# Cross attention's chain, setup products, division and weight split re-placed, and the last scaling done on VectorE alone

## The chip, the cores and the metric

The kernel runs on one core of one Trainium2 chip. The metric is the device time of one execution in microseconds (us), the slowest core's, which here is the only one. Three runs of the kernel before gave 744.47 to 745.14 us, median 744.66.

## What is computed

Two transformer layers in a row, on x of shape 2 x 1024 x 256 in float32 with a context of 2 x 77 x 256:

```python
# layer 0, 16 heads of 16, scale 64 ** -0.5
x = attention(ln(x), ln(x), Wq1, Wkv1, Wo1, bo1) + x      # self attention, 1024 keys
x = attention(ln(x), context, Wq2, Wkv2, Wo2, bo2) + x    # cross attention, 77 keys
lin, gelu = split(ln(x) @ Wff1 + bff1)                    # 256 -> 2 x 1024
x = (lin * gelu * sigmoid(1.702 * gelu)) @ Wff2 + bff2 + x
# layer 1, one head of 256, keys and values from the context
Q, K, V = x @ Wq.T + bq, ctx @ Wk.T + bk, ctx @ Wv.T + bv
out = softmax(Q @ K.T / 16) @ V @ Wfc.T + bfc
x = norm_w * rms_normalised(out + x)
```

## The kernel before, in words

The order of the work is written out by hand: each engine has its own program, and the engines meet at semaphores. "TensorE" is PE in the rows, "VectorE" DVE, "ScalarE" ACT, "GpSimd" POOL, "SyncE" SP. The tokens are 16 tiles of 128 rows, or 4 blocks of 512. Everything stays in SBUF but for the parts of the projected queries and keys, which go to DRAM and come back in another layout (`q_parts`, `k_parts`).

**Self attention** has 8 groups (one group is 4 heads of one batch entry) of 16 steps each. TensorE makes scores for the row maxima (L760), which VectorE reduces (L1562), then transposed scores (L926), ScalarE takes their exponential (L1324) and TensorE weighs the values with it (L938). It reads the values from the tile `v1`. GpSimd has almost nothing to do here: from the fourth half group on it splits the maxima into two float16 parts (L663 to L667), for which it waits 13 times.

**Cross attention** has 8 groups of 4 units. I number the units 0 to 31, unit 4 G + d being `cross_unit(G, d)`. In a unit TensorE makes transposed scores (L1034, `scores_t2`) and, 6 units ahead (`S2_LEAD`), a tile of scores for the maxima (L1023, `scores_2`). There are 32 such tiles. VectorE reduces each (L1764, `reduce_2`), and TensorE makes no tile before the one ahead of it is reduced. After every fourth tile VectorE splits the group's maxima (L1568, L1570) and TensorE turns them (L1061, `turn_max_2`) in the third unit of a group. ScalarE takes the exponential (L1379), TensorE weighs the values (L1043) in a group's first and third unit and turns the result back (L1054) in the second and fourth, and VectorE divides it by the sums (`attended`, L1713 and L1719).

Between these pieces stand two more kinds of work, which the change moves:

- The **chain** (`chain(n, b)`): after attention n of batch entry b come 2 transposes of the attention's output (L713), 8 output products (L901), each added to x by VectorE (L1657) with its statistics (L1531, L1532), and for each block a transpose of the normalised tokens (L713), in self attention's chain followed by 2 projections of the queries (L727). A `yield` ends one piece. The table `PIECES` says how many pieces a unit gets. The normalisation between (root in 12 small instructions, then four `tok` writes, L1540) is drawn out over the units by `tick(3)`, three instructions each time. TensorE takes half of a unit's pieces in the middle of the unit (rounded down) and the rest at its end.
- The **setup products** of layer 1 (`final_setup`, `setup`, L843): kT and vT (two each), g1 (two), cb, and vw (one for each batch entry, after which SBUF holds V @ Wfc.T + bfc). Seven of them are made just ahead of the score tiles numbered in `SETUP_TILES`, in columns 312 onward of the score tiles' PSUM banks, which the score tile leaves free (`SPARE`). The two vw products are 256 columns wide, more than is free there, so they wait for all score tiles and come after units 28 and 30 (`SETUPS`).

```python
PIECES = ((2, 1, 1, 1), (1, 1, 1, 1), (0, 0, 0, 0), (0, 0, 0, 0),
          (0, 0, 1, 1), (2, 1, 2, 1), (1, 1, 0, 1), (0, 1, 0, 0))
SETUP_TILES = (10, 14, 15, 17, 19, 21, 23)
SETUPS = {(7, 0): 1, (7, 2): 1}
```

**The feed-forward part** works on products of split operands: each float32 weight is split into a high and a low part. GpSimd does this for the second weight (`wff2_hi`, `wff2_lo`, L628, L630, four pairs of instructions), after the bias of the cross attention and once self attention no longer reads `v1`, where `wff2_hi` lies; then, once all query parts are stored, for the first (L637, L639, eight pairs). The first block's input is split by ScalarE (`x_high(0)`, L1364, after unit 28) and VectorE (`x_low(0)`, L1753, after unit 29).

**The tail** is layer 1's attention over 77 keys, the residual (L1848), sums of squares on ScalarE (L1454), a reciprocal root on VectorE (`l1_root`, 12 instructions) and the scaling. Block 0 is scaled on ScalarE (`l1_scale`, L1460) and GpSimd (L672), blocks 1 to 3 on VectorE (`l1_final`, L1860). SyncE stores the blocks in the order 0, 1, 3, 2 (L575).

## Time and profile before

| what | value |
|---|---|
| median of three runs | 744.66 us |
| the profiled execution's own time | 745.36 us |
| its span, first to last instruction | 743.5 us |
| TensorE busy | 670.9 us (90%) |
| VectorE busy | 534.5 us (72%) |
| ScalarE busy | 486.2 us (65%) |
| GpSimd busy | 92.8 us (12%) |
| chain that ended last | TensorE 66%, VectorE 18%, ScalarE 9% |

The profile is of one execution. The span is shorter than the execution's own time by the 1.9 us that lie around it. Busy shares are averages over stages with different limits, so the stages are read one by one. The granted clock is TensorE's: 1.00 is 2.4 GHz, 0.50 is 1.2 GHz. The chain that ended last is followed back from the last instruction, at each step to what released it.

### The profile page before, as it was taken

To read this page: it belongs to the slowest core of one execution; us is meant where nothing else is said; L and a number is where in the kernel's file an instruction comes from. 1 tells how busy PE (TensorE), PEld (TensorE's weight loads), DVE (VectorE), ACT (ScalarE), POOL (GpSimd) and SP (SyncE) were. 2 spreads that over 40 slices of the span, in tenths; PEclk is the share of its full clock that TensorE was granted. 3 is DMA by queue.
4 is the path that set the end of the run, shared out by engine and by line. 5 is a ranking of instruction groups with operands and counts; after the bars stand their busy time and mean duration, and the time that the engine had idled before them with its cause. 6 is when DMAs were issued, how large, how long until landed. Compare 5 with 4: busy or idle time off the path is not lost.

```text
span 743.5 us, 11151 instructions
## 1 busy us (share of the span) xinstructions
PE 670.9 (90%) x4072; PEld 321.4 (43%) x4072; DVE 534.5 (72%) x925; ACT 486.2 (65%) x845; POOL 92.8 (12%) x144
## 2 busy tenths in 40 slices
PE   4989799999999999999999888989989989999991
PEld 2644122222222222222224344344547878888881
DVE  6778999999999999999984538453753844343357
ACT  3542399999999999999998653444674223332374
POOL 2080800000000000000000201570000050000001
PEclk9999599999999999999999999865999999999996
DMA  9557450202020110101000031120000000000003
GB/s 305 195 178 240 100 185 5 69 1 71 1 72 2 44 30 1 30 2 30 1 2 1 29 89 27 55 69 24 2 2 1 0 1 1 1 1 1 1 0 113
DMA packets 35113, 36.87 MB, mean 50 GB/s; under 512 B 6132, under 2 KB 28276, under 8 KB 34804
## 3 DMA queue, kind: packets, MB, share of 16 engines
q1 hardware_dynamic: 33904, 35.87, 15.2%
q0 software_dynamic: 1024, 0.24, 0.3%
q8 instruction: 32, 0.52, 0.3%
q14 instruction: 21, 0.17, 0.1%
q10 hardware_dynamic: 132, 0.07, 0.0%
HBM read 23.09 MB, written 12.74 MB: 48 GB/s over the span
## 4 chain that ended last, share of the span: by engine, by line
PE 66%; DVE 18%; ACT 9%; issue 5%; DMA 1%; SPq 0%; DVEq 0%; ACTq 0%
PE ps L938 15%; PE ps L926 10%; DVE mm L1562 7%; PE ps L727 6%; ACT probs L1324 6%; PE ps L1127 4%; PE ps L1128 4%; PE ps L1129 4%; PE ps L760 4%; PE ps L713 3%; PE ps L1043 3%; PE ps L901 2%; PE ps L1143 2%; PE ps L1142 2%; PE ps L1144 2%
## 5 line engine op out<-in xcount | busy, mean ns | idle before, releaser
L1324 ACT ACTIVATE probs<-ps,unfit 128x512 f32<-128x512 f32 x512 | 311.7, 691 | 29.1 <-PE ps L926 24.6
L1562 DVE TENSOR_REDUCE mm<-ps 128x2 f32<-128x1024 f32 x256 | 299.5, 1219 | 14.4 <-PE ps L760 10.4
L926 PE MATMUL ps<-stack 50*128 50x512 f16 x512 | 147.2, 389 | 7.2 <-ACT probs L1324 1.2
L938 PE MATMUL ps<-probs,v 128*32 128x512 f32 x1024 | 137.6, 609 | 2.7 <-ACT outT L1329 2.7
L760 PE MATMUL ps<-stack 48*128 48x512 f16 x512 | 109.1, 392 | 12.6 <-DVE mm L1562 6.6
L926 PEld LDWEIGHTS ps<-stack 50*128 50x128 f16 x512 | 36.9, 93 | 172.9 <-ACT probs L1324 164.8
L1424 ACT ACTIVATE early<-ps,cols 128x512 f32<-128x512 f32 x32 | 22.1, 690 | 93.1 <-PE ps L1129 93.1
L1822 DVE SCALAR_TENSOR_TENSOR hid<-ps,cols,early 128x512 f32<-128x512 f32 x32 | 24.0, 750 | 74.3 <-PE ps L1129 74.3
L621 POOL TENSOR_TENSOR x<-x,rows 128x512 f32<-128x512 f32 x24 | 30.9, 1314 | 164.8 <-PE ps L1129 91.4
L1127 PE MATMUL ps<-x_hi,wff_hi 128*128 128x512 f32 x128 | 51.3, 401 | 0.1
L1379 ACT ACTIVATE probs<-ps,unfit 96x1024 f32<-96x1024 f32 x32 | 35.5, 1108 | 23.2 <-PE ps L1034 23.2
L1128 PE MATMUL ps<-x_lo,wff_hi 128*128 128x512 f32 x128 | 50.3, 393 | 0.0
L1129 PE MATMUL ps<-x_hi,wff_lo 128*128 128x512 f32 x128 | 50.2, 392 | 0.0
L760 PEld LDWEIGHTS ps<-stack 48*128 48x128 f16 x512 | 26.1, 94 | 54.3 <-DVE mm L1562 30.5
L713 PE MATMUL ps<-ident,tok 128*128 128x128 f32 x160 | 27.0, 313 | 18.2 <-DVE tok L1540 13.9
L663 POOL TENSOR_SCALAR mu<-mm 128x16 f32<-128x16 f32 x13 | 3.3, 254 | 286.9 <-DVE mm L1578 286.9
L938 PEld LDWEIGHTS ps<-probs,v 128*32 128x32 f32 x1024 | 20.6, 108 | 40.7 <-issue 30.8
L1142 PE MATMUL ps<-wff_hi,hid_hi 128*128 128x256 f32 x128 | 37.2, 290 | 0.0
L1143 PE MATMUL ps<-wff_lo,hid_hi 128*128 128x256 f32 x128 | 36.6, 286 | 0.0
L1144 PE MATMUL ps<-wff_hi,hid_lo 128*128 128x256 f32 x128 | 36.2, 283 | 0.0
L901 PE MATMUL ps<-wo,wkv 128*128 128x256 f32 x128 | 33.6, 398 | 2.2 <-DVE x L1657 1.6
L1764 DVE TENSOR_REDUCE mm<-ps 128x8 f32<-128x616 f32 x32 | 25.3, 790 | 11.5 <-PE ps L1023 11.2
(168 smaller groups left out, 863.8 us busy)
## 6 DMA issues: line engine op xcount, KB each, us to landing
v_groups<-early SPq DMA_DIRECT2D x8, 512.0 KB, 3.4
stack<-q_parts SPq DMA_DIRECT2D x64, 64.0 KB, 2.0
v<-v_groups SPq DMA_DIRECT2D x8, 512.0 KB, 4.1
x<-in_x SPq DMA_DIRECT2D x4, 512.0 KB, 7.6
q_parts<-probs SPq DMA_DIRECT2D x8, 256.0 KB, 3.8
k_parts<-probs SPq DMA_DIRECT2D x8, 256.0 KB, 2.5
stack<-k_parts SPq DMA_DIRECT2D x16, 128.0 KB, 2.5
stack<-q_parts SPq DMA_DIRECT2D x64, 32.0 KB, 1.9
```

What stands on the lines that cost most here:

```text
L713: mm_ = eng.transpose(ps[:, turn_bank(phase, blk, c), P * t:P * t + P], src, ident[:, :])
L760: mm_ = eng.matmul(ps[:, 2 * s_slot(G, j, i) + tile, :], qs[rows_i, slot, half, q, P * t:P * t + P], stack[rows_i, SLOTS + slot, q, BLK * ...
L926: eng.matmul(ps[:, st_bank(n), :], stack[rows_of(tile, KROWS), SLOTS + slot, q, P * kc:P * kc + P], qs[rows_of(tile, KROWS), slot, half, q ...
L938: mm_ = eng.matmul(ps[32 * h:32 * h + 32, PV, :], v1[:, G % 2, kc, 32 * h:32 * h + 32], probs[:, k % 2, h, :], start=(kc == 0), stop=(kc = ...
L1127: eng.matmul(ps[:, bank, :], wh, xh[:, c, :], start=(c == 0), stop=False)
L1128: eng.matmul(ps[:, bank, :], wh, xl[:, c, :], start=False, stop=False)
L1129: mm_ = eng.matmul(ps[:, bank, :], wl, xh[:, c, :], start=False, stop=(c == NC - 1))
L1142: eng.matmul(out, hh, w2h, start=(f == 0), stop=False)
L1143: eng.matmul(out, hh, w2l, start=False, stop=False)
L1144: mm_ = eng.matmul(out, hl, w2h, start=False, stop=(f == FC - 1))
L1324: eng.activation(probs[:, k % 2, HEADS[h], :], ps[:, st_bank(n), :], ACT.Exp, scale=unfit[:, 0:1]).then_inc(exp_done, 1)
L1562: eng.tensor_reduce(dst, ps[:, 2 * slot:2 * slot + 2, :], AX.X, ALU.max).then_inc(s_red, 1)
```

## The change

Six edits:

1. `PIECES` gives one piece to each unit that has any. A piece leaves unit 0 for unit 8; in the second chain the eight output products come one per unit in units 20 to 27, and the two last transposes in units 29 and 31 in place of 27 and 29. `x_high(0)` comes after unit 30 and `x_low(0)` after unit 31.
2. The setup products come ahead of the tiles 14 to 24, in units 8 to 18, one each. vw is made in halves of 128 columns so that all fit in the spare columns; there are 11 products in place of 9.
3. In a unit VectorE divides the attention's output before the three instructions of `tick(3)`, and no further `tick(3)` follows a division.
4. GpSimd splits the second weight in self attention, between the loads of k2 and the first maxima. `wff2_hi` lies over `p1T`, which only the tail uses, and `p1T` is no longer cleared at the start. The tail's products over `p1T` read 77 rows in place of 96.
5. VectorE alone scales all four blocks: block 0 after the residual of block 3, then one root for blocks 1 to 3 and their twelve instructions.
6. SyncE stores the blocks in the order 0 to 3.

```diff
-        wff2_hi, wff2_lo = over("wff2_hi", "v1", [P, FC, D], F32R), over("wff2_lo", "wff2", [P, FC, D], F32R)
+        wff2_lo = over("wff2_lo", "wff2", [P, FC, D], F32R)
...
+        wff2_hi = over("wff2_hi", "p1T", [P, FC, D], F32R)
...
-        PIECES = ((2, 1, 1, 1), (1, 1, 1, 1), (0, 0, 0, 0), (0, 0, 0, 0),
-                  (0, 0, 1, 1), (2, 1, 2, 1), (1, 1, 0, 1), (0, 1, 0, 0))
-
-        SETUP_TILES = (10, 14, 15, 17, 19, 21, 23)
-        SETUPS = {(7, 0): 1, (7, 2): 1}
+        PIECES = ((1, 1, 1, 1), (1, 1, 1, 1), (1, 0, 0, 0), (0, 0, 0, 0),
+                  (0, 0, 1, 1), (1, 1, 1, 1), (1, 1, 1, 1), (0, 1, 0, 1))
+
+        SETUP_TILES = range(14, 25)
...
-            for n, blk in enumerate((0, 1, BLOCKS - 1, 2)):
-                if n == 0:
-                    eng.wait_ge(l_out, TPB)
-                else:
-                    eng.wait_ge(l_last, TPB * n)
+            for blk in range(BLOCKS):
+                eng.wait_ge(l_last, TPB * (blk + 1))
...
                 if n == 1:
-
-                    eng.wait_ge(w_in["wff"], 32)
-                    eng.wait_ge(pv_done, 16 * GROUPS)
-                    for f in range(0, FC, 2):
...
+                    eng.wait_ge(w_in["wff"], 32)
+                    for f in range(0, FC, 2):
+                        hi, w = wff2_hi[:, f:f + 2, :], wff2[:, f:f + 2, :]
+                        eng.tensor_copy(hi, w).then_inc(w2_split, 1)
...
-                eng.wait_ge(s2_red, KC // 2 * GROUPS)
                 for b in range(B):
-                    setup(k, CTX, D, [(vT[:, c, cut[b]], wfcT[:, c, :]) for c in range(NC)]
-                          + [(ones[0:1, 0:CTX], rows[0:1, ROW_BFC, :])])
-                    k += 1
-                    yield
+                    for n in (slice(0, P), slice(P, D)):
+                        setup(k, CTX, P, [(vT[:, c, cut[b]], wfcT[:, c, n]) for c in range(NC)]
+                              + [(ones[0:1, 0:CTX], rows[0:1, ROW_BFC, n])])
+                        k += 1
+                        yield
...
-                    if (G, d) == (LAST, 0):
+                    if (G, d) == (LAST, 2):
                         x_high(0)
...
             def attended_2(G, half):
                 attended(2 * GROUPS + 2 * G + half, MISC)
-                tick(3)
...
-                tick(3)
-                advance(pieces, PIECES[G][d] // 2)
                 if d == 1 and G >= 1:
                     attended_2(G - 1, 1)
                 if d == 3:
                     attended_2(G, 0)
-                advance(pieces, PIECES[G][d] - PIECES[G][d] // 2)
+                tick(3)
+                advance(pieces, PIECES[G][d])
...
-                    if (G, d) == (LAST, 1):
+                    if (G, d) == (LAST, 3):
                         x_low(0)
...
-            l1_root(1, 2)
-            l1_final(1, 2)
-            l1_root(2, BLOCKS)
-            l1_final(last, 3)
-            l1_final(2, 3)
+            l1_final(0, 1)
+            l1_root(1, BLOCKS)
+            for blk in range(1, BLOCKS):
+                l1_final(blk, 2)
```

Three places of the order, before and now. Line numbers of the change differ from those before.

The first is VectorE in units 0 and 1. Before, from the output product added in the middle of unit 0 to the reduction of the next score tile in unit 1 (`x<-ps,x` is the sum of an output product and x, `rstd` and `var` the root, `tok` the normalised tokens, `mm` the maxima):

```order
L1657 TENSOR_TENSOR x<-ps,x 128x256
L1531 BN_STATS st<-x 128x6
L1532 BN_AGGR mv<-st 128x2
L1514 TENSOR_TENSOR var<-rstd 128x4
L1514 TENSOR_TENSOR var<-var,half_var 128x4
L1517 SCALAR_TENSOR_TENSOR rstd<-var,rstd 128x4
L1657 TENSOR_TENSOR x<-ps,x 128x256
L1531 BN_STATS st<-x 128x6
L1532 BN_AGGR mv<-st 128x2
L1540 TENSOR_SCALAR tok<-x,mv,rstd 128x256 x3
L1764 TENSOR_REDUCE mm<-ps 128x2x2x2
```

Now, from the same output product:

```order
L1637 TENSOR_TENSOR x<-ps,x 128x256
L1511 BN_STATS st<-x 128x6
L1512 BN_AGGR mv<-st 128x2
L1494 TENSOR_TENSOR var<-rstd 128x4
L1494 TENSOR_TENSOR var<-var,half_var 128x4
L1497 SCALAR_TENSOR_TENSOR rstd<-var,rstd 128x4
L1744 TENSOR_REDUCE mm<-ps 128x2x2x2
L1548 TENSOR_SCALAR mpart<-mm 128x2x16
L1550 SCALAR_TENSOR_TENSOR mpart<-mm,mpart 128x2x16
L1520 TENSOR_SCALAR tok<-x,mv,rstd 128x256 x3
```

One output product with its statistics and three `tok` writes no longer stand ahead of that reduction.

The second is TensorE in units 10 and 11, where no chain pieces are. Before (`ps<-stack,k` the transposed scores, `ps<-k,stack` the score tile, `identh,mpart` the turned maxima, `probs,v` the weighing, `ctxT,early` a setup product, `ident,outT` the turned output):

```order
L1034 MATMUL ps<-stack,k 96x512 x2
L1023 MATMUL ps<-k,stack 128x78 x8
L1061 MATMUL ps<-identh,mpart 96x128
L1043 MATMUL ps<-probs,v 32x512 x4
L1034 MATMUL ps<-stack,k 96x512 x2
L843 MATMUL ps<-ctxT,early 128x154 x2
L1023 MATMUL ps<-k,stack 128x78 x8
L1054 MATMUL ps<-ident,outT 128x128 x4
```

Now:

```order
L1022 MATMUL ps<-stack,k 96x512 x2
L831 MATMUL ps<-ctxT,early 128x154 x2
L1011 MATMUL ps<-k,stack 128x78 x8
L1049 MATMUL ps<-identh,mpart 96x128
L1031 MATMUL ps<-probs,v 32x512 x4
L1022 MATMUL ps<-stack,k 96x512 x2
L831 MATMUL ps<-ctxT,early 128x154 x2
L1011 MATMUL ps<-k,stack 128x78 x8
L1042 MATMUL ps<-ident,outT 128x128 x4
```

Unit 10 has a setup product too, ahead of its score tile; so have all units from 8 to 18, where before every second one had.

The third is TensorE at the end of cross attention, units 29 to 31 up to the feed-forward part's first product (`ps<-x_hi...`). Before, from unit 29:

```order
L1034 MATMUL ps<-stack,k 96x512 x2
L1054 MATMUL ps<-ident,outT 128x128 x4
L713 MATMUL ps<-ident,tok 128x128 x8
L1034 MATMUL ps<-stack,k 96x512 x2
L1043 MATMUL ps<-probs,v 32x512 x4
L843 MATMUL ps<-early,vT 77x256 x2
L843 MATMUL ps<-rows,ones 77x256
L1034 MATMUL ps<-stack,k 96x512 x2
L1054 MATMUL ps<-ident,outT 128x128 x4
L1043 MATMUL ps<-probs,v 32x512 x4
L1127 MATMUL ps<-x_hi_55,wff_hi 128x512
```

Now, units 29 to 31:

```order
L1022 MATMUL ps<-stack,k 96x512 x2
L1042 MATMUL ps<-ident,outT 128x128 x4
L702 MATMUL ps<-ident,tok 128x128 x8
L1022 MATMUL ps<-stack,k 96x512 x2
L1031 MATMUL ps<-probs,v 32x512 x4
L1022 MATMUL ps<-stack,k 96x512 x2
L1042 MATMUL ps<-ident,outT 128x128 x4
L702 MATMUL ps<-ident,tok 128x128 x8
L1031 MATMUL ps<-probs,v 32x512 x4
L1114 MATMUL ps<-x_hi_54,wff_hi 128x512
```

The vw products are gone from here, and the second transpose of the normalised tokens (`ident,tok`) has moved from unit 29 to unit 31, the last.

## Rows read from the trace of the kernel before

**Rows 1.** The page's first line
```profile
span 743.5 us, 11151 instructions
```

**Rows 2.** Busy time by stage, columns in the first line
```profile
core 0: us, PE busy (x) PEld busy (x) DVE busy (x) ACT busy (x) POOL busy (x), PEclk, DMA share, GB/s
450.70:462.30 11.60, 8.65 (x62) 4.90 (x63) 10.72 (x42) 4.96 (x6) 2.63 (x2) 0.87 0.10 24
462.30:482.80 20.50, 19.06 (x108) 8.19 (x107) 10.33 (x27) 10.72 (x15) 10.11 (x10) 0.82 0.13 41
490.00:520.40 30.40, 28.81 (x165) 13.88 (x166) 11.66 (x25) 13.15 (x18) 11.88 (x13) 0.50 0.13 35
520.40:545.00 24.60, 21.61 (x178) 12.48 (x174) 20.04 (x70) 14.75 (x19) 0.00 (x0) 0.99 0.01 2
555.20:715.40 160.20, 155.86 (x912) 136.88 (x909) 72.94 (x149) 55.83 (x99) 10.55 (x8) 0.99 0.00 1
715.40:743.50 28.10, 12.23 (x75) 10.16 (x73) 19.94 (x73) 15.69 (x60) 2.78 (x4) 0.80 0.22 75
```

**Rows 3.** The same view, two short stretches of units 0 to 7
```profile
459.60:462.30 2.70, 2.70 (x15) 1.58 (x12) 2.33 (x11) 1.35 (x2) 0.69 (x1) 0.50 0.03 6
473.00:479.50 6.50, 6.50 (x27) 2.24 (x25) 0.95 (x2) 3.22 (x5) 6.13 (x7) 0.50 0.13 33
```

**Rows 4.** Timeline of TensorE: start, duration, line, operands, [idle before]
```profile
458.09 0.32 PE L1023 MATMUL ps<-k,stack 48*128 48x78 f16 x8 [2.15 <-DVE mm L1764]
...
489.86 0.23 PE L1061 MATMUL ps<-identh,mpart 128*96 128x128 f16 x1 [1.74 <-DVE tok L1719]
...
554.18 1.06 PE L1043 MATMUL ps<-probs,v 96*32 96x512 f32 x8 [0.62 <-ACT probs L1379]
```

**Rows 5.** One line's instructions on VectorE (ns, min/median/max, first and last start)
```profile
L1570 DVE SCALAR_TENSOR_TENSOR mpart<-mm,mpart x11: 174/193/1183, 77.0 to 540.5; 128x32 f16<-128x32 f32 x8, 128x16 f16<-128x16 f32 x3
```

**Rows 6.** Timeline of GpSimd, start of the first weight's split
```profile
487.09 0.61 POOL L637 CAST wff_hi<-wff 128x512 fp32r<-128x512 f32 x1 [5.23 <-DMA q_parts<-stack]
```

**Rows 7.** Chain of waits: start, us, work
```profile
483.25 0.72 PE ps L843 x4
...
506.16 1.32 PE ps L843 x4
...
507.86 1.04 PE ps L1054 x4
...
546.28 1.60 PE ps L843 x6
```

**Rows 8.** Timeline of ScalarE: exponentials of units 10 and 19
```profile
487.51 1.11 ACT L1379 ACTIVATE probs<-ps,unfit 96x1024 f32<-96x1024 f32 x1 [0.63 <-PE ps L1034]
...
520.88 1.12 ACT L1379 ACTIVATE probs<-ps,unfit 96x1024 f32<-96x1024 f32 x1
```

**Rows 9.** Timeline of VectorE at the end of cross attention
```profile
545.68 1.06 DVE L1540 TENSOR_SCALAR tok<-x,mv,rstd 128x256 f32<-128x256 f32 x3
...
549.48 1.22 DVE L1753 TENSOR_TENSOR x_lo<-xT,x_hi 128x1024 fp32r<-128x1024 f32 x1
```

**Rows 10.** Timeline of VectorE in the tail
```profile
730.24 0.64 DVE L1509 TENSOR_SCALAR half_ms<-ms 128x4 f32<-128x4 f32 x1
...
732.90 1.67 DVE L1860 SCALAR_TENSOR_TENSOR x<-x,rms,rows 128x256 f32<-128x256 f32 x4
...
736.90 3.26 DVE L1860 SCALAR_TENSOR_TENSOR x<-x,rms,rows 128x256 f32<-128x256 f32 x8
```

**Rows 11.** Timeline of SyncE's queue, load of the second weight
```profile
92.91 0.47 SPq L507 DMA_DIRECT2D wff<-in_Wff  x1
```

**Rows 12.** DMA issues: name, KB each, us to landing
```profile
wff<-in_Wff SPq DMA_DIRECT2D x1, 1024.0 KB, 10.4
```

**Rows 13.** Timeline of VectorE in self attention
```profile
118.41 0.18 DVE L1580 TENSOR_TENSOR mm<-mm 128x16 f32<-128x16 f32 x1
```

**Rows 14.** Groups by line: us in total, mean ns, idle before
```profile
L630 POOL TENSOR_TENSOR wff_lo<-wff,wff_hi 128x512 fp32r<-128x512 f32 x4 | 5.1, 1270 | 0.3
```

45 lines of the change are left out of this document (14 added, 31 removed).

## The prediction

> **What bounds the kernel now.** I read busy time by stage first. The span is 743.5 us [rows 1]. The feed-forward stretch of 160.2 us has TensorE busy for 155.86 us at full clock, and the change touches nothing in it. Self attention gains one thing, the second weight's split on GpSimd. That leaves cross attention (450.7 to 555.2) and the tail after 715.4. The reader should see in [rows 2] that three stages of cross attention have three limits. In units 0 to 3 VectorE is busy 10.72 of 11.60 us. From 490.0 to 520.4 TensorE is busy 28.81 of 30.40 us, but at a granted clock of 0.50, which is 1.2 GHz. From 520.4 to 545.0 both are near full (21.61 and 20.04 of 24.60). So the largest thing at stake is not an amount of work but 30.4 us at half clock, with 2.7 and 6.5 us more at half clock before it [rows 3].
>
> I then looked at what TensorE did ahead of the falls. Before 459.6 it had stood 2.15 us, waiting for a score tile's reduction. Before 490.0 it had stood 1.74 us, waiting for the maxima and the division [rows 4]. In that second wait lies one VectorE instruction, the low half of the maxima, that took 1183 ns where the median is 193 [rows 5]. It fell into the time just after GpSimd had started to split the first weight at 487.09 [rows 6]. TensorE did not come back to full clock until a transpose of the chain, at 520.4. The trace shows only that order of events; that the waits cause the falls is my reading.
>
> **The change part by part.**
>
> *Units 0 to 8, one piece each.* Between two reductions of score tiles VectorE has three `tok` writes (1.06 in [rows 9]), one addition of an output product and its statistics fewer, an estimated 2 us, about the size of the 2.15 us wait. VectorE's total work until unit 3 is the same, at 92% busy, so most of this wait will spread over the next units and not vanish. What can go is the 2.7 us stretch at half clock behind it: at full clock it is 1.35 us shorter. I take -1.4. Best case, both half-clock stretches go (half of 9.2 is 4.6) with the wait: -6.8. Worst case, the transpose that moves to unit 6 now finds its four `tok` writes just being made, 4 x 0.35 = 1.4: +1.4. Dividing first brings the division forward by three small instructions, about 0.5 us, in units with a root under way. TensorE waits on it there only in a group's third unit; I count it within these bounds.
>
> *Units 8 to 19, a setup product in each to 18.* Units 10 to 19 run from 487.51 to 520.88, 33.4 us for nine units [rows 8], the last with a transpose. How much work moves in: from unit 11 on there were four wide products, and there will be four wide ones and four halves. A wide one costs 0.72 at full and 1.32 at half clock; a vw whole costs 1.60 [rows 7]. A half has six records of 128 columns; the transposes of 128 columns take 1.04 / 4 = 0.26 each at half clock [rows 7], so a half is 1.56 there, and about 0.85 at full. Four halves add 6.2 at half clock, 3.4 at full.
> At full clock the stretch would hold 28.81 / 2 + 3.4 = 17.8 us of TensorE's work, two group waits of 1.74 (3.5) and a wait of 0.62 for an exponential in every second unit (2.8) [rows 4], together 24.1, so -9.3. At half clock all the way it grows by the halves: +6.2. These are the ends. Which is nearer? What stood ahead of the fall was a pause of 1.74 us in unit 10 with no other work for TensorE. Now unit 10 has a product of 0.72 to fill the same wait, and the slow VectorE instruction should be quick there. The reason is that GpSimd starts the first weight only when the last query parts are stored, 487.09 [rows 6], and their projection moves from unit 7 to unit 8, so unit 9's maxima come first. The collision then meets unit 13's maxima, whose wait also has a product in it. I expect full clock for most of the stretch with one fall like the 6.5 us at 473.0 [rows 3], which costs 3.3: -9.3 + 3.3 = -6.0.
>
> *Units 20 to 31.* The same VectorE work is spread evenly. Two vw products go (3.20), but ScalarE is busy there too with its copies, and I count half, -1.6. Against it, the last block's transpose now stands in unit 31: its four `tok` writes (1.4), and then `x_low(0)` (1.22) [rows 9], come behind the last division, and the feed-forward part waits for both. Before, TensorE had its last output turned at 554.18 - 0.62 = 553.56, and 1.06 us of weighing from 554.18 on ended the stage [rows 4], so 1.7 us in all. Now come a division (an estimated 0.7), the `tok` writes (1.4), the part of the transpose left after the last of them (about 0.7 of twice 0.52, [rows 7]) and the weighing (1.06), 3.9. That is +2.2. Sum +0.6, ends -3.2 and +2.2.
>
> *The tail.* One root goes (from 734.57 to 736.90, 2.33), four scalings come (1.67), and the instruction of 0.64 that ran beside GpSimd's product becomes about 0.2 like other small ones [rows 5]: -2.33 + 1.67 - 0.44 = -1.1 [rows 10]. Block 0 leaves later, but the last two blocks leave one behind the other as before, so the last store is not later relative to the last scaling. Ends -1.6 (ScalarE's four scalings also gone from ahead of its squares) and 0 (three stores closer together).
>
> *The second weight's split.* Its load is issued at 92.91 and lands 10.4 us later [rows 11, 12], and four pairs of 1.27 and 0.61 take 7.5 us [rows 6, 14], so it runs from about 103.3 to 111. VectorE's next work on SBUF operands begins at 118.41 [rows 13], and GpSimd's own first maxima come with the fourth half group, much later. Cover: over 5 us. I count 0, ends 0 and +1 (a slowed VectorE instruction in a stage that ScalarE bounds). At its old place nothing waited for it: the next split waited for stored parts until 487.09 anyway. The `p1T` clearing and the 77 rows change no duration on the path: 0.
>
> **Sum.** -1.4 - 6.0 + 0.6 - 1.1 = -7.9. Against the profiled execution's 745.36 this is 737.5. The median of the runs is 0.7 lower, so I forecast **736.8**.
>
> **Rivals.**
> *A, no half clock left in units 10 to 19.* For it: TensorE has a product in every wait. Against it: three falls in 40 us before. -1.4 - 9.3 + 0.6 - 1.1 = -11.2, 733.5; with the first term's best case, 728.
> The Trainium skill, "TensorE: Matmul & The Clock Gate", Part 1, says that the clock is low after idleness and is released by sustained activity. By that rule a denser TensorE is released early and rival A is the outcome. The trace agrees on the falls, which follow waits, and speaks against the second half: 28.81 of 30.40 us busy and no release [rows 2]. So A does not get the largest share.
> *B, the fall only comes later.* Units 11 to 14 at full clock save about 4.5 us, and the four halves still fall in the half-clock part (+6.2). Sum -1.4 + 1.7 + 0.6 - 1.1 = -0.2: no change. With one of the halves at full clock it is -1 to -4.
> *C, slower: the half-clock stretch stays as long and has four more products in it.* Its place is units 11 to 19 on TensorE, its price +6.2. It decides as soon as the clock falls before unit 12, since nothing but chain work was seen to end such a stretch. Sum -1.4 + 6.2 + 0.6 - 1.1 = +4.3, 749.0. For it: half-clock TensorE stayed busy and at 0.50 with products in every second unit.
> *D, one piece per unit does nothing*, because VectorE is the limit in units 0 to 3 and 20 to 27 and its work is unchanged. The clock is then drawn as before. Its times are those of B and C.
>
> **How the numbers follow.** About 0.2% (1.5 us) is what a measurement of this kernel can tell from no change. The forecast's case (-4 to -9.5) gets 0.37, A 0.18, B 0.20 (half of it within 0.2%, half slightly faster), C with what is slower in D 0.25. Faster is 0.37 + 0.18 + 0.10 = 0.65, same 0.10, slower 0.25. The range reaches into A and C: 730.0 to 749.5. The forecast's own case spans 735 to 741.
>
> **What would show each step.** The 2.15 us wait of TensorE gone and the half-clock stretch at 459.6 with it; the share of 0.50 between units 10 and 19 well under half; the slow maxima instruction in unit 13 and not in unit 9; a wait of TensorE for `tok` in unit 31 of 1 to 2 us; the last scaling ending about 1 us earlier relative to the last residual; self attention as long as before. Wrong would be: the half-clock stretch still 25 us or more, or a new half-clock stretch at the start of the feed-forward part.

## The result, and the profile after

The changed kernel was slower: median 750.38 us (748.30 to 751.27, eight runs) against 743.40 us (738.93 to 745.14, eight runs) of the kernel before, ratio 1.0107, 95% interval 1.0077 to 1.0137. That is 13.6 us over the forecast of 736.8 and 0.9 us over the end of the range, 749.5. Its profiled execution took 750.86 us (span 748.8), against 745.36 (span 743.5) before. Runs of one kernel differ mostly by how long TensorE ran at half clock (one kernel below took 730.82 us at a mean granted clock of 0.974 and 746.57 us at 0.947), so I set medians beside what each profile shows of the clock; the ratios leave out runs over 1.5% above the fastest of their kernel, which leaves two of the four runs of e5 below, and of e2 and e3 only one each, so that they have no ratio.

Busy time by stage of the changed kernel, columns as in [rows 2]:

```profile
451.90:462.30 10.40, 8.26 (x74) 4.83 (x73) 9.78 (x38) 5.44 (x7) 2.65 (x2) 1.00 0.10 28
462.30:482.80 20.50, 17.75 (x113) 7.70 (x112) 12.87 (x34) 11.76 (x16) 2.64 (x2) 0.92 0.15 50
492.90:526.60 33.70, 31.20 (x168) 15.47 (x170) 9.75 (x24) 11.73 (x15) 9.95 (x11) 0.50 0.09 28
526.60:549.60 23.00, 21.39 (x178) 11.62 (x172) 18.87 (x61) 14.87 (x20) 0.00 (x0) 0.99 0.01 2
557.80:561.00 3.20, 3.20 (x12) 1.34 (x12) 0.30 (x1) 2.21 (x4) 0.00 (x0) 0.50 0.00 0
559.70:719.80 160.10, 155.91 (x901) 136.51 (x898) 72.22 (x146) 54.61 (x93) 10.54 (x8) 0.97 0.00 1
719.80:748.80 29.00, 13.46 (x85) 11.39 (x83) 19.98 (x67) 15.43 (x63) 0.00 (x0) 0.76 0.22 73
```

Units 0 to 3 now run at full clock (1.00, before 0.87 in [rows 2]), and the stretch behind them is at 0.92, before 0.82. But the long half-clock stretch has not shortened: it was 30.4 us and is 33.7. A new one of 3.2 us stands at the start of the feed-forward part. What stands ahead of the long one, and in it, is on TensorE's timeline (start, duration, work, [idle before]):

```profile
489.97 0.66 PE L1042 MATMUL ps<-ident,outT 128*128 128x128 f32 x4
495.40 0.66 PE L1022 MATMUL ps<-stack,k 50*96 50x512 f16 x2 [4.78 <-DMA stack<-mT]
...
507.90 1.14 PE L831 MATMUL ps<-early,vT 128*77 128x128 f32 x4
508.97 0.71 PE L831 MATMUL ps<-rows,ones 1*77 1x128 f32 x2
...
524.07 1.97 PE L702 MATMUL ps<-ident,tok 128*128 128x128 f32 x8
```

The wait of 1.74 us at unit 10 [rows 4] is gone. In its place TensorE stands 4.78 us at unit 12, for the DMA that brings group 3's maxima (`mT`) into the stack. Where these maxima were is seen on ScalarE's timeline (their copy), in SyncE's queue, and in the chain of waits (start, us, work):

```profile
487.77 0.27 ACT L1359 ACTIVATE mT<-ps 64x128 f16<-64x128 f32 x1 [0.58 <-PE ps L1049]
```
```profile
481.10 4.60 SPq L440 DMA_DIRECT2D q_parts<-stack  x2
485.74 7.02 SPq L456 DMA_DIRECT2D stack<-q_parts  x12
492.81 1.28 SPq L528 DMA_DIRECT2D stack<-mT  x2
```
```profile
488.90 1.54 SPq L456 DMA_DIRECT2D stack<-q_parts  x1
```
```profile
493.47 1.89 DMA stack<-mT
```

They were ready at 488.04 (487.77 + 0.27) and issued from 492.81: SyncE first issues twelve query loads, eight of them only after the last query parts are stored. One of these twelve alone, the line at 488.90, took 1.54 us to issue, where most take about 0.4; what held it is not shown. The same load in the kernel before, where TensorE came to unit 12 at half clock and did not wait:

```profile
490.80 1.28 SPq L531 DMA_DIRECT2D stack<-mT  x2
```

The span is split here at events that both timelines show; "unit" is the start of that unit's exponential on ScalarE:

| stretch | before | after | difference | forecast |
|---|---|---|---|---|
| up to unit 0 | 451.15 | 452.37 | +1.22 | 0 |
| unit 0 to 9 | 34.63 | 32.04 | -2.59 | -1.4 |
| unit 9 to 12 | 10.15 | 11.70 | +1.55 | |
| unit 12 to 19 | 24.95 | 30.57 | +5.62 | with the line above -6.0 |
| unit 19 to the feed-forward part | 34.29 | 33.00 | -1.29 | +0.6 |
| feed-forward part to the last residual | 174.96 | 176.08 | +1.12 | 0 |
| last residual to the last scaling | 10.03 | 9.61 | -0.42 | -1.1 |
| last scaling to the end | 3.34 | 3.43 | +0.09 | 0 |
| sum | 743.5 | 748.8 | +5.30 | -7.9 |

At the end of cross attention, VectorE and TensorE in unit 31:

```profile
552.46 0.16 DVE L1497 SCALAR_TENSOR_TENSOR rstd<-var,rstd 128x4 f32<-128x4 f32 x1
554.96 0.26 DVE L1693 RECIPROCAL rec<-ps 128x16 f32<-128x16 f32 x1 [2.34 <-PE ps L1042]
555.26 0.42 DVE L1699 TENSOR_TENSOR tok<-ps,rec 128x256 f32<-128x256 f32 x1
555.60 1.37 DVE L1520 TENSOR_SCALAR tok<-x,mv,rstd 128x256 f32<-128x256 f32 x4
```
```profile
556.15 1.74 PE L702 MATMUL ps<-ident,tok 128*128 128x128 f32 x8 [1.22 <-DVE tok L1520]
```

The root was done at 552.62. Then VectorE stood 2.34 us for the division's input, with the four `tok` writes queued behind the division, because the third edit puts the division first. TensorE waited 1.22 us for them.

The tail on VectorE, which answers to [rows 10]:

```profile
734.10 1.66 DVE L1825 SCALAR_TENSOR_TENSOR x<-ps,r,x 128x256 f32<-128x256 f32 x4
735.68 1.66 DVE L1837 SCALAR_TENSOR_TENSOR x<-x,rms,rows 128x256 f32<-128x256 f32 x4
738.07 0.17 DVE L1489 TENSOR_SCALAR ms<-ss 128x12 f32<-128x12 f32 x1 [0.72 <-ACT sq L1441]
...
740.53 4.84 DVE L1837 SCALAR_TENSOR_TENSOR x<-x,rms,rows 128x256 f32<-128x256 f32 x12
```

One root is gone, but VectorE now stands 0.72 us for ScalarE's squares.

### The profile page after: what moved, and what is told of

Same layout as the page of the kernel before. It is cut to its first block, busy times and chain, and to the rows that moved or that the text cites. A ratio compares the mean times of both kernels' runs of the same rounds, so it can differ in the third digit from the quotient of the medians.

```text
span 748.8 us, 11160 instructions
## 1 busy us (share of the span) xinstructions
PE 674.0 (90%) x4084; PEld 323.9 (43%) x4084; DVE 533.8 (71%) x919; ACT 484.8 (65%) x841; POOL 88.4 (12%) x139
## 4 chain that ended last, share of the span: by engine, by line
PE 66%; DVE 16%; ACT 10%; issue 5%; DMA 1%; SPq 1%; DVEq 0%; ACTq 0%
PE ps L926 15%; PE ps L914 10%; DVE mm L1542 7%; PE ps L716 6%; ACT probs L1311 5%; PE ps L1114 4%; PE ps L1115 4%; PE ps L1116 4%; PE ps L749 4%; PE ps L702 3%; PE ps L889 3%; PE ps L1031 2%; PE ps L1131 2%; PE ps L1129 2%; PE ps L1130 2%
## 5 line engine op out<-in xcount | busy, mean ns | idle before, releaser
L702 PEld LDWEIGHTS ps<-ident,tok 128*128 128x128 f32 x160 | 20.4, 155 | 28.3 <-issue 19.7
```

The source lines that it names most:

```text
L702: mm_ = eng.transpose(ps[:, turn_bank(phase, blk, c), P * t:P * t + P], src, ident[:, :])
```

## Experiments

All sixteen ran beside runs of the kernel before on the same chip; "before" is the median of those. The last column is from each run's profile.

| run | median (range), runs | before | ratio, 95% interval | unit 12 to 19, us |
|---|---|---|---|---|
| e1 maxima ahead of the last loads | 750.29 (747.47-751.12), 5 | 743.44 | 1.010 (1.0065-1.0134) | 30.5 |
| e2 maxima from ScalarE | 743.59 (730.82-746.57), 4 | 743.44 | - | 28.3 |
| e3 setup placement alone, on before | 749.24 (735.60-751.03), 4 | 743.44 | - | 30.6 |
| e4 second chain as before | 754.93 (751.13-758.49), 4 | 743.44 | 1.0169 (1.0112-1.0225) | 30.6 |
| e5 e2 and GpSimd in two lots | 739.51 (733.57-747.55), 4 | 743.79 | 0.9876 (0.9817-0.9936) | 19.1 |
| e6 eight transposes added | 741.50 (738.53-744.23), 10 | 743.79 | 0.9973 (0.9943-1.0003) | 22.2 |
| e7 three products added | 742.10 (738.58-746.22), 10 | 743.79 | 0.9991 (0.9957-1.0025) | 23.3 |
| e8 division after the root | 746.95 (744.86-748.68), 10 | 743.79 | 1.0054 (1.0028-1.0080) | 30.6 |
| e9 e5, e8 and e6 together | 733.91 (728.49-736.42), 6 | 743.86 | 0.9870 (0.9828-0.9912) | 19.2 |
| e10 setup placement undone | 741.99 (739.46-744.85), 10 | 743.86 | 0.9979 (0.9953-1.0005) | 24.5 |
| e11 eight transposes on before | 744.90 (739.80-745.61), 12 | 743.86 | 1.0010 (0.9983-1.0038) | 23.0 |
| e12 transposes twice | 732.68 (729.40-742.06), 6 | 743.86 | 0.9853 (0.9812-0.9893) | 28.2 |
| e13 two lots, on before | 741.34 (738.25-745.30), 12 | 743.62 | 0.9980 (0.9957-1.0003) | 24.2 |
| e14 three edits (e5 and e8) | 731.32 (728.08-733.46), 5 | 743.62 | 0.9835 (0.9809-0.9862) | 18.7 |
| e15 e14, setup placement undone | 736.80 (731.85-742.99), 10 | 743.62 | 0.9911 (0.9878-0.9943) | 17.9 |
| e16 both repairs on before | 734.03 (728.62-740.15), 6 | 744.12 | 0.9863 (0.9809-0.9916) | 16.3 |

### e1 and e2: is the new wait the queue's?

```diff
 load_q2(4, (1,))
-load_q2(5, (1,))
 load_max_2(3)
+load_q2(5, (1,))
```

> The changed kernel with one move in SyncE's queue: the two loads of group 3's maxima go ahead of the last four query loads. In the changed kernel TensorE stood 4.78 us at unit 12 for these maxima, which were issued at 492.81 although ScalarE had copied them some 4 us before. Theory Q (the wait is the queue's, and the half clock from 492.9 on follows from it): the load is issued some 1.7 us earlier, the wait shrinks to about 3 us, and the time falls by 1.7 us at least, to about 748.7. The clock still falls behind a 3 us wait. Theory F (TensorE loses its clock in these units by itself, whatever it waits for): the clock falls at the same place, and the time falls by the same 1.7 us or less. Rival W (the wait is for the copy or the product of the maxima, not for the queue): the wait stays above 4 us and the time at 750.4. A new wait is possible at the first tile that reads the four query loads, unit 14's: under 1 us.

```diff
 # ScalarE, behind its copy of the maxima; SyncE no longer has load_max_2(3)
+if G == 3:
+    eng.wait_ge(m_copied, 2 * GROUPS + G + 1)
+    n = PARTS * HP * KC
+    for tile in range(HT):
+        eng.dma_start(stack[max_rows(tile), Q2_SLOT[G % 4], :, :].rearrange("i h n -> i (h n)"),
+                      mT[n * tile:n * tile + n, G % 2, :]).then_inc(m2_in[G % 4], 16)
```

> The changed kernel, but the two loads of group 3's maxima are issued by ScalarE itself right behind its copy of them, in unit 10, and not by SyncE behind its query loads. Theory Q: the wait of 4.78 us at unit 12 falls under 1 us. If the clock then holds, units 12 to 18 run in some 20 us in place of 31, and the time falls by 10 us or more, to 740 or less; if it falls at another wait before unit 14, the time falls by about the 4 us of the wait, to 746. Theory F says the latter: the stretch at 0.50 begins in these units anyway and ends only at the chain's transpose in unit 18. Rival W: nothing changes, the wait is still over 4 us.

TensorE in e1, then in e2 with a window of e2, and GpSimd and VectorE in e2:

```profile
493.29 0.66 PE L1022 MATMUL ps<-stack,k 50*96 50x512 f16 x2 [2.51 <-DMA stack<-mT]
```
```profile
498.07 0.23 PE L1048 MATMUL ps<-identh,mpart 128*96 128x128 f16 x1 [1.42 <-DVE tok L1704]
```
```profile
498.20:518.60 20.40, 20.40 (x108) 9.80 (x109) 6.28 (x15) 7.32 (x10) 4.03 (x5) 0.51 0.09 22
```
```profile
495.43 1.27 POOL L622 TENSOR_TENSOR wff_lo<-wff,wff_hi 128x512 fp32r<-128x512 f32 x1
```
```profile
495.58 1.16 DVE L1553 TENSOR_SCALAR mpart<-mm 128x32 f16<-128x32 f32 x1
496.77 0.53 DVE L1555 SCALAR_TENSOR_TENSOR mpart<-mm,mpart 128x32 f16<-128x32 f32 x1
```

The wait is the queue's: 4.78 became 2.51 with four loads fewer ahead of it, and at unit 12 of e2 no wait for it is left. Rival W is out. But e1's time did not move. Its clock fell all the same, and 1.7 of the 2.1 us that its profile had gained at unit 12 were given back in the feed-forward part, where more of it ran at half clock (from the first product to the last residual 177.75 us, in the changed kernel 176.08). In e2 the clock held through units 12 and 13 and fell at unit 14, behind the next wait: two small VectorE instructions took 1.16 and 0.53 us in place of 0.18 and 0.19 while GpSimd was splitting the first weight. This is the same collision as the 1183 ns of [rows 5], one group of maxima later. The kernel before had this second one too, at half clock, with a wait of 1.21 us behind it at 503.39:

```profile
501.39 1.00 DVE L1568 TENSOR_SCALAR mpart<-mm 128x32 f16<-128x32 f32 x1
```

One run of e2 took 730.82 us at a mean clock of 0.974, so in all likelihood the clock can hold there.

The Trainium skill, "SBUF — State Buffer", section "SBUF: two separate sides", says that VectorE and GpSimd share one pair of ports as an exclusive lock, and that the loser waits for the other's whole instruction; on VectorE it counts only instructions in a two-port mode or with two inputs in SBUF. The times here agree: the slow instruction ended at 496.74, just behind the GpSimd subtraction that ended at 496.70, and the excess, 1.16 - 0.18 = 0.98 us, is under one such subtraction (1.27). The instruction has one input, and no run here shows its mode.

### e5: take the collision away as well

```diff
 for f in range(FC):          # GpSimd, the first weight's split
+    if f == FC // 2:
+        eng.wait_ge(m_step, 3 * ON_DVE + 2 * 5)   # group 4's maxima are split
```

> The kernel of the run before last but one, in which ScalarE issues the loads of group 3's maxima, with one more edit: GpSimd splits the first weight in two lots of four pairs, and begins the second lot only once VectorE has split group 4's maxima. Without this edit the profile showed the next wait of TensorE at unit 14: 1.42 us at 498.07, behind two VectorE instructions of 1.16 and 0.53 us that otherwise take 0.18 and 0.19 and ran while GpSimd was splitting, and the clock fell at about 498.2 and stayed low for 20.5 us. Theory G (this collision makes the wait, and the wait the fall): the two instructions take about 0.2 each, the wait is under 0.3 us, the clock holds through units 12 to 18 in most runs, and the time is 731 to 735. Theory F (the clock falls in these units anyway): the wait goes, the stretch at 0.50 stays 17 to 31 us long, and the time is within 2 us of 743.6.

Units 9 to 19 of e5:

```profile
484.40:510.80 26.40, 24.01 (x228) 13.08 (x227) 15.04 (x38) 15.37 (x21) 14.68 (x16) 1.00 0.24 65
```

Clock 1.00 throughout. Two of four runs took 733.8 and 733.6 us, the others 745.3 and 747.6. Theory G's mechanism is shown in the profile, which is of the run of 733.78 us; "in most runs" was not.

### e3, e10 and e15: the placement of the setup products

e3 puts the second edit alone on the kernel before; e10 undoes it alone in the changed kernel; e15 undoes it in the kernel of three edits (below), with GpSimd's first lot held back behind group 3's maxima as well, as in e13.

```diff
-SETUP_TILES = (10, 14, 15, 17, 19, 21, 23)    # e3; reversed in e10 and e15
-SETUPS = {(7, 0): 1, (7, 2): 1}
+SETUP_TILES = range(14, 25)
```

> The kernel before with the placement of the setup products alone: ahead of tiles 14 to 24, vw in four halves, nothing behind units 28 and 30. Theory C of the prediction (the half-clock stretch stays as long and holds four more products): where the clock falls at unit 10 or before as it did, the stretch up to the transpose of unit 18 grows from 30.4 us to about 36, and the products gone from units 28 and 30 give back up to 3: the time rises by 3 to 6 us over the kernel before. Theory D (dense TensorE work holds the clock): the product in unit 10 covers the 1.74 us wait there, the clock holds, and the time falls by 5 us or more. Rival: the pieces and the queue are the whole loss, and this stands within 1 us of the kernel before.

> The changed kernel with its second edit alone undone: the setup products ahead of the tiles 10, 14, 15, 17, 19, 21 and 23, and the two whole vw products after units 28 and 30. Theory C of the prediction (four more products lie in the half-clock stretch and cost 6 us there): the wait of over 4 us at unit 12 stays, the stretch at 0.50 is 27 to 31 us long in place of 34, and the time falls by 6 less up to 3 for the products at the end, 3 to 6 us: 744.5 to 747. Rival Q (the 4.78 us wait is what costs, not the products): 750 within 1.

The half-clock stretch of e3, and then of e10, with the wait of TensorE ahead of the latter:

```profile
485.50:523.00 37.50, 37.50 (x202) 18.98 (x195) 12.76 (x31) 14.77 (x19) 11.64 (x13) 0.50 0.10 28
```
```profile
488.20:518.90 30.70, 26.25 (x154) 13.22 (x156) 10.79 (x24) 12.56 (x17) 13.57 (x15) 0.50 0.15 40
```
```profile
486.59 0.23 PE L1055 MATMUL ps<-identh,mpart 128*96 128x128 f16 x1 [0.75 <-DVE tok L1706]
```

Theory C holds. e3 has the changed kernel's time without any of its other edits, and without its 4.78 us wait: there the clock fell at unit 10 already, behind a wait of 1.10 us, and the setup products after it were paid at half clock. e10 falls by 8.4 us although it still waits 3.30 us at unit 12. From its unit 12 to 19 it takes 24.5 us against 30.6. That is 6.1 us, and the prediction had priced rival C at 6.2. The median came out under the 744.5 to 747 that I expected; where the rest was gained is open. The clock of e10 fell at 488.2, ahead of the long wait, when TensorE had stood only 0.40 and 0.75 us in unit 10. (One run of e3 took 735.60 us at a clock of 0.968: the fall is likely, not certain.)

> The same three edits on the changed kernel with its setup placement undone (seven products in every second unit, two whole vw products after units 28 and 30). Theory H (the new placement costs only where the clock is low, and holds the clock where it is high): this one loses the clock more often and is slower than the kernel of three edits in its fast group, 736 or more. Theory C alone (products in these units cost, and do nothing for the clock): it is as fast or faster, 730 to 733.

With the waits mended, the sign is the other: e15 is slower than e14 in the median, 736.80 against 731.32. Where the clock holds, the placement itself is worth little: in both profiles it held over nearly all of units 9 to 19, e15 took 0.9 us less there (25.20 against 26.05) and 1.0 us more from unit 19 to the feed-forward part, and the spans differ by 1.7 us. The rest of the difference goes with the clock: five of e15's ten runs had a mean clock of 0.956 or less, no run of e14 had under 0.967. That fits a placement that helps to keep the clock, as the prediction assumed, but it is not shown: e5, with the new placement, lost it in two of four runs (0.950 and 0.945), and e16, with the old one, in one of six (0.956). What is shown is that the placement is paid dearly once the clock is lost.

### e6, e7 and e11: what gives the clock back?

```diff
+if (G, d) == (3, 1):          # end of unit 13; e11: (2, 3), unit 11
+    eng.wait_ge(rest_done, len(PROJ))
+    for t in range(2 * TPB):
+        eng.transpose(ps[:, CHAIN + t // TPB, P * (t % TPB):P * (t % TPB) + P], ident[:, :], ident[:, :])
```

e7 has three pairs of products of `wkT` with `ctxT` in that place.

> The changed kernel with eight transposes of the identity added on TensorE at the end of unit 13, into two PSUM banks that nobody reads; their results are used by nothing. In all profiles so far the half-clock stretch of units 12 to 18 ended in the chain's eight transposes of unit 18. Theory T (work of that kind, or an uninterrupted stretch of it, gives the clock back): the stretch begins at 492.9 as before, ends within unit 13 or 14, is 7 to 14 us long in place of 34, and the time falls by (34 - 10) / 2 less 1 to 2 for the transposes, 10 us: about 740. Theory U (the clock comes back by its own time, whatever is done): the stretch stays over 27 us, and the time rises by the 2 us of the transposes, to 752.

> The twin of the kernel with eight added transposes: in the same place, three products of the setup kind (two matrices of 128 x 128 against 154 columns each, 1.39 us a piece at half clock) in place of the transposes, some 4 us of uninterrupted float32 work. Theory T1 (any dense work gives the clock back): as there, the stretch shrinks to 7 to 14 us, and the time is about 741. Theory T2 (it is the transposes that do it): the stretch stays over 27 us, and the time rises by the 4 us, to 754.

e6's added transposes and the windows around them; then e7's added products:

```profile
503.16 1.41 PE L1070 MATMUL ps<-ident 128*128 128x128 f32 x8
```
```profile
493.60:503.80 10.20, 7.99 (x44) 4.60 (x44) 2.43 (x5) 2.79 (x3) 9.80 (x11) 0.50 0.17 46
503.80:518.70 14.90, 14.49 (x137) 8.01 (x137) 7.45 (x21) 8.56 (x12) 0.04 (x1) 1.00 0.12 30
```
```profile
499.31 2.54 PE L1071 MATMUL ps<-ctxT,early 128*128 128x154 f32 x12
```

In both the stretch is 10.2 us in place of 33.7, and ends inside the added work; the times fall by 8.9 and 8.3 us. Neither kind is special (T2 is out), and in these two kernels it is no matter of time alone (U is out). Work that nobody uses made the changed kernel faster. There TensorE was busy for 31.20 of 33.70 us at 0.50 without release. The Trainium skill ("TensorE: Matmul & The Clock Gate", Part 1) says that sustained activity releases the clock. By that rule it should have come back early here, and it did not. What ends such a stretch stays open. At the end of the long one in the changed kernel, and of those in e6 and e7, TensorE had just made or was making a block of float32 products with 128 x 128 weights: the chain's eight transposes (1.97 us at 524.07), eight added ones, or three added pairs. But two later profiles speak against a rule from that. TensorE in e12, which has eight transposes at the ends of units 12 and 15 (its slowest run, 742.06 us), and then in e15, which has none added:

```profile
492.16 0.79 PE L832 MATMUL ps<-kT,early 128*128 128x154 f32 x4 [1.00 <-DMA stack<-q_parts]
...
494.41 1.97 PE L1071 MATMUL ps<-ident 128*128 128x128 f32 x8
```
```profile
493.80:510.80 17.00, 17.00 (x87) 10.30 (x83) 5.16 (x13) 5.38 (x7) 8.61 (x9) 0.50 0.18 45
```
```profile
499.50:502.90 3.40, 3.40 (x30) 2.29 (x33) 1.86 (x5) 1.54 (x3) 3.24 (x5) 0.50 0.32 82
```

In e12 the first eight transposes did not end the stretch that had just begun; it lasted 17.0 us and ended behind the second eight, which began at 507.63. In e15 a stretch ended after 3.4 us, over the ordinary work of units 15 and 16. So in the changed kernel the added work gave the clock back (all twenty runs of e6 and e7 are under its fastest, 748.30 us), but such a block is neither always enough nor always needed.

> The kernel before, with nothing changed but eight transposes of the identity, which nobody reads, at the end of unit 11. Theory T (an uninterrupted stretch of float32 work gives the clock back): the stretch at 0.50, which begins at 490.0 in unit 10, ends within 10 to 14 us in place of 30.4, and the time falls by (30.4 - 12) / 2 less 2 us for the transposes at half clock, 7 us: 736 to 738. Theory U (what freed the clock in the changed kernel belongs to that kernel): no gain, 745.

TensorE in e11, and the granted clock between:

```profile
489.69 0.23 PE L1061 MATMUL ps<-identh,mpart 128*96 128x128 f16 x1 [1.75 <-DVE tok L1723]
...
494.91 1.89 PE L1082 MATMUL ps<-ident 128*128 128x128 f32 x8
...
503.00 0.23 PE L1061 MATMUL ps<-identh,mpart 128*96 128x128 f16 x1 [1.73 <-DVE tok L1723]
```
```profile
489.85:496.70 6.85, 6.85 (x35) 4.04 (x34) 2.13 (x5) 1.95 (x3) 6.61 (x8) 0.50 0.32 88
496.70:503.10 6.40, 4.32 (x48) 2.20 (x47) 4.02 (x8) 3.81 (x4) 5.24 (x6) 1.00 0.01 2
503.10:520.20 17.10, 16.71 (x100) 8.15 (x99) 5.66 (x13) 7.84 (x12) 0.00 (x0) 0.51 0.09 26
```

The clock came back, and TensorE ran into the collision of unit 14 at full speed: 1.73 us of waiting, and the clock was gone for 17.1 us more. No gain, against my expectation. The two waits stand one behind the other. Curing one handed the fall to the next here.

### e13 and e16: the same two repairs on the kernel before

```diff
+    if f % (FC // 2) == 0:     # GpSimd waits for group 3's, then group 4's maxima
+        eng.wait_ge(m_step, 3 * ON_DVE + 2 * (4 + f // (FC // 2)))
```

> The kernel before with one edit: GpSimd begins the first four pairs of the first weight's split only once VectorE has split group 3's maxima (unit 9), and the other four once it has split group 4's (unit 13). In the kernel before, the maxima instruction of 1183 ns and a wait of TensorE of 1.74 us stood ahead of the fall at 490.0, and with eight transposes added the clock came back at 497 and fell again at 503, behind a second wait of 1.73 us at unit 14. Theory G (the collision with GpSimd makes both waits, and they the falls): both waits go under 1 us, no or a shorter half-clock stretch, time 731 to 738. Theory F (the clock falls there anyway, the units have too little uninterrupted work): the waits shrink, the stretch stays near 30 us, 742 to 745.

TensorE in e13:

```profile
489.44 0.23 PE L1063 MATMUL ps<-identh,mpart 128*96 128x128 f16 x1 [0.75 <-DVE tok L1721]
...
495.42 0.66 PE L1036 MATMUL ps<-stack,k 50*96 50x512 f16 x2 [2.86 <-DMA stack<-mT]
```

The time, 741.34 us, is no change clear of noise (0.9957 to 1.0003) and lies between the two theories' ranges. With the collision gone, the kernel before meets the wait that the changed kernel met. Here too the load of the maxima was late all along, hidden by a TensorE that came later and slower.

> The kernel before with the two repairs and nothing of the change: GpSimd's split in two lots behind VectorE's maxima, and the loads of group 3's maxima issued by ScalarE. With the lots alone the wait of 1.74 us at unit 10 went to 0.75, TensorE stood 2.86 us at unit 12 for the maxima's load instead, the clock fell there at 494, and the time was 741.3. Theory Q+G (these two waits make the half-clock stretch): the wait at unit 12 goes under 0.5 us, the stretch is gone or short in most runs, the median is 733 to 738. Rival F: the units 12 to 18 of the kernel before are too thin to hold the clock (every second unit has no setup product), it falls there in most runs, and the median is 740 to 744.

Units 9 to 19 of e16:

```profile
482.80:506.40 23.60, 19.61 (x201) 10.25 (x200) 13.00 (x32) 15.35 (x22) 14.72 (x16) 1.00 0.23 65
```

35.10 us before, 23.60 now. So the collisions and the late load together are the cause of the half-clock stretch in the kernel before as well, and rival F is out: five of the six runs had a mean clock of 0.967 or more, the sixth (740.15 us) had 0.956.

### e4 and e8: the end of cross attention

e4 gives the second chain and `x_high`, `x_low` their old places; e8 puts `tick(3)` ahead of the division.

```diff
-(0, 0, 1, 1), (1, 1, 1, 1), (1, 1, 1, 1), (0, 1, 0, 1))    # e4
+(0, 0, 1, 1), (2, 1, 2, 1), (1, 1, 0, 1), (0, 1, 0, 0))
```
```diff
+tick(3)                                                     # e8
 if d == 1 and G >= 1:
     attended_2(G - 1, 1)
 if d == 3:
     attended_2(G, 0)
-tick(3)
```

> The changed kernel with the second chain of the kernel before: its PIECES from group 5 on, x_high after unit 28 and x_low after unit 29. The last transposes are back in units 27 and 29. The changed kernel waited 1.22 us for tok in unit 31 and had 3.2 us at half clock from 557.8 on, over the first feed-forward products. Theory E (both come from the transpose in unit 31): both go, and the time falls by 1.2 + 0.8 + 1.6 = some 3 us, to about 747.5. Rival: VectorE bounds units 20 to 27 and two pieces in units 20 and 22 cost what the end gives back; then it stays at 750.4 within 0.7.

> The changed kernel with its third edit undone in part: in each unit the three instructions of the root or the tok writes come ahead of the division again. In the changed kernel VectorE had the root done at 552.6 and then stood 2.34 us in unit 31 for the division's input, with the four tok writes queued behind it, and TensorE waited 1.22 us for them. Theory V: the tok writes are made in that idle time, the wait of 1.22 us goes, and with it the half-clock stretch of 3.4 us that begins at 557.8; the time falls by 1.2 + 1.7 = 3 us, to 747.5, if the maxima's units do not pay for it. Rival: the divisions come 0.5 us later in the units with a root, TensorE waits for them in every third unit of groups 5 to 7, and the time stays within 1 us of 750.4.

TensorE in e4, then in e8:

```profile
546.38 0.23 PE L1049 MATMUL ps<-identh,mpart 128*96 128x128 f16 x1 [1.90 <-DVE tok L1699]
...
554.31 1.64 PE L702 MATMUL ps<-ident,tok 128*128 128x128 f32 x8 [1.22 <-DVE tok L1520]
```
```profile
554.58 0.76 PE L702 MATMUL ps<-ident,tok 128*128 128x128 f32 x5 [0.81 <-DVE tok L1520]
```

e4 missed both ways: 4.6 us slower than the changed kernel. The wait of 1.22 us is still there, in unit 29, so with the division first it comes at either place. And with the division first the old pieces cost a wait of 1.90 us in unit 26 (0.93 in the kernel before, 1.03 in the changed one). With that order, the second chain as the change has it was a gain. e8 came out at the expected time, 3.4 us faster, but with only a part of its mechanism: three of the four `tok` writes were made in the idle time, the fourth stayed behind the division, and in unit 31 the 1.22 us became 0.81 and did not go. The kernel before, with the old order and the transpose in unit 29, had no wait there. So the order and the place each bring a wait. The half clock at the start of the feed-forward part went in e8's profile.

### e9, e12 and e14: a version that beats both

e14 is the changed kernel with e2's loads, e5's two lots and e8's order. e9 adds e6's transposes, and e12 adds them at the ends of units 12 and 15 in place of 13.

> The changed kernel with four edits together: ScalarE issues the loads of group 3's maxima, GpSimd splits the first weight in two lots, the root and the tok writes come ahead of the division, and eight transposes of the identity are added at the end of unit 13. The first two alone gave 733.7 in two runs and 745 to 747.6 in two others. Theory: the transposes end a half-clock stretch that begins before unit 13, where it does, so the slow runs come down by some 8 us, to 738; in the good runs they cost 1 us; the order of the division gives 3 us in all of them. Median 732 to 736. Rival: in the slow runs the clock falls behind unit 13, and the transposes give nothing; then the runs stay in two groups, near 731 and near 743.

> The kernel of four edits, but the eight transposes stand at the end of unit 12 and again at the end of unit 15. If in the slow runs of that kernel the clock falls behind unit 13, this one is the faster by some 3 us in them and the two groups of times close up, median 732 to 735. If the clock is seldom lost there, this one is 1 us slower for eight more transposes.

> The kernel of four edits without the eight added transposes: ScalarE's loads, GpSimd's two lots, the root ahead of the division. If the transposes were what kept the slow group of times away, the runs fall in two groups again, near 730 and near 743, as the first two edits alone did (733.7 and 746). If not, the median is 732 to 733, 1 us under the kernel of four edits.

Units 9 to 19 of e14:

```profile
483.10:509.10 26.00, 23.95 (x228) 13.02 (x227) 15.02 (x37) 15.32 (x21) 14.70 (x16) 1.00 0.24 66
```

e14 is the best that was run: 731.32 us, 1.65% under the kernel before (ratio 0.9835, 0.9809 to 0.9862). All five of its runs lie between 728.08 and 733.46, so the transposes were not needed to keep times like e5's 745 and 748 away. Whether e8's order did, or four runs of e5 and five of e14 are too few to tell, stays open. e12's median is 1.2 us under e9's, within the spread of both, and one of its runs took 742.06: no verdict between them. That run's profile shows what was late next: at unit 12 TensorE stood 1.00 us for a query load (the line at 492.16 above), and the clock fell at 493.8.

## Why the prediction was wrong, point by point

**What bounds the kernel.** Right: the half-clock stretch was the largest thing at stake. That waits of TensorE start it was "my reading"; e2, e5, e11, e13 and e16 bear it out. How long a wait must be is not shown: e10's clock fell behind 0.75 us, e16's held through the same wait.

**Units 0 to 8.** Forecast -1.4, measured -2.6. The 2.15 us wait and the half-clock stretch at 459.6 went, as said. Smaller waits for reductions, up to 0.93 us, took its place in the next units. The worst case came too: in unit 6 the transposes waited 0.93 and 0.94 us for their `tok` writes. The half clock of 6.5 us around 473.0 lasted only about 3.4 us (475.7 to 479.1), which the -1.4 did not count. The +1.22 before unit 0 seems to be none of the change's: half clock around 445, in the last work of self attention, lasted about 7 us in this execution and about 3.4 before. In e3 and e10 the same place came out at 450.3 and 449.2.

**Units 8 to 19: the step that failed.** The prediction took -6.0 because "unit 10 has a product of 0.72 to fill the same wait, and the slow VectorE instruction should be quick there". Both came true; unit 10 had no wait left. The error was the next sentence, "I expect full clock for most of the stretch". I removed a wait and did not ask what is late next. SyncE's load of group 3's maxima was late by some 5 us for a TensorE that no longer waited at unit 10. It was issued at 490.80 before and at 492.81 after. Of these 2.0 us, 0.9 come from the last stores, which moved with the projections to unit 8 (GpSimd, which waits for them, started at 487.09 and at 487.98); the query load of 1.54 us makes the rest. I had used that later store only in my favour, for the collision. TensorE stood 4.78 us, the clock fell there, and rival C followed at its own price: +5.62 from unit 12 to 19, and with the 1.55 ahead of it +7.2 where -6.0 was forecast. That is the whole of the miss in the span, -7.9 against +5.30. From unit 12 to 19 there were three wide products in both kernels. Four halves at 1.14 + 0.71 less their overlap, 1.71 each, make 6.8; waits of 1.21 and 0.39 us of the kernel before were gone, -1.6. Together +5.2 of the +5.62. The prediction had sized a half at 1.56. The trace it was read from held the collision at unit 13's maxima already (the 1.00 us at 501.39), with 1.21 us of waiting behind it.

**Rival C's condition**, "as soon as the clock falls before unit 12", was met at about 492.8, in the wait for unit 12. My sentence "nothing but chain work was seen to end such a stretch" was true of cross attention in the trace and wrong as a rule: e6 and e7 ended it with other work, and in e15 one ended after 3.4 us without any.

**Units 20 to 31.** Forecast +0.6, measured -1.3. The gain of the even pieces was sized too low (e4 points that way, though it moves `x_high` and `x_low` too), and the loss in unit 31 was there: `tok` waited for with 1.22 us, within "1 to 2". I had put it down to the place of the transpose; e4 and e8 show that the order of division and root brings it as well. The new half-clock stretch at the feed-forward part, named as a sign of being wrong, came with it.

**The feed-forward part.** Forecast 0, measured +1.12: the half clock at its start, and a stretch near 605 of about 7 us where before there was one of about 3.4 near 601. The work is the same (155.91 us busy, 155.86 before).

**The tail.** Forecast -1.1, measured -0.42. The instruction count was right. The 0.72 us wait for ScalarE's squares was missing from the sum; with it the sum gives -0.4.

**The second weight's split.** Right: its last subtraction began at 110.52 and took 1.27 us, well before VectorE's next work on SBUF at 118, and it cost nothing visible. The collision did not move to unit 13's maxima in the changed kernel, since the 4.78 us wait carried that unit to the end of GpSimd's work, which ended at 503.24 (its slowest maxima instruction, at 503.01, took 269 ns). Once the wait was mended, in e2, it came where the prediction had put it.

**The chances.** 0.25 for slower was too little. Three waits in a row hung on other queues (SyncE, GpSimd), and the forecast needed the clock to survive all of them. And 1.5 us was too little as what a measurement can tell: eight runs of the kernel before spread over 6.2 us.

## What to carry to other kernels

Where one wait sets a clock fall, list every later wait that it hides before pricing its removal: follow each load that the next units read back to its place in its queue. In a stretch that may run at half clock, added TensorE work costs nearly double if the clock is lost (a wide product 1.39 us in place of 0.79), so move work in only once the waits there are gone. For a small load behind many others in one queue, try the engine that made its data: here that took away the wait of 4.78 us (e2).

## What the runs showed of the hardware that I had not expected

- TensorE stayed at 0.50 for 33.7 us while busy for 31.20 of them, and for 37.5 us in e3, busy for all of it. Eight useless transposes (e6) or three product pairs (e7) ended such a stretch after 10.2 us, but eight transposes in e12 did not end one, and one in e15 ended after 3.4 us without them.
- A VectorE instruction of 0.18 us on a 128 x 32 tile took 1.16 us beside GpSimd's split. With the 0.53 us of the next one, that was enough to cost TensorE 1.42 us of waiting, and 20.4 us at half clock followed (e2).
- Short waits went before a fall in one kernel and not in another: TensorE had stood 0.40 and 0.75 us in unit 10 when e10's clock fell at 488.2, and 0.34 and 0.75 us in the same unit of e16, where it stayed at 1.00.
- The same kernel keeps or loses the clock from run to run: e3 took 735.60 us once, at a mean clock of 0.968, and 748.74 to 751.03 in the other three runs, at 0.943 to 0.945.
